# The second layer norm's statistics spread over three engines in a fused attention and feed-forward kernel

## What is computed

```
x = x + tanh(g_xattn) * attention(layernorm(x), ctx)      # 8 heads of 64, 77 context rows
y = fixed_quant(layernorm(x), 8, 4)                       # second layer norm: mean and variance of each row
h = relu(fixed_quant(y @ w1q.T + b1q, 8, 4))              # 1024 wide
x = x + tanh(g_ffn) * (h @ w2q.T + b2q)

layernorm(x) = (x - mean(x)) / sqrt(var(x) + 1e-5)
```

## Time and profile before

| what | value |
|---|---|
| median of 3 runs | 121.85 us (121.33, 121.85, 123.11) |
| span of the profiled execution | 119.5 us |
| TensorE, VectorE, ScalarE, GpSimd busy | 95%, 82%, 64%, 74% of the span |
| granted TensorE clock | full (2.4 GHz) in all slices |

### The profile page before, as it was taken

The page is one execution under the profiler, slowest core; times in us unless marked ns, Lnnn a source line. Parts: engine busy times, 40 slices in busy tenths (PEclk is TensorE's granted clock), DMA queues, the critical chain, the costliest instruction groups (busy, mean ns, idle before and its releaser), DMA issues.

```text
span 119.5 us, 2896 instructions
## 1 busy us (share of the span) xinstructions
PE 113.6 (95%) x1012; PEld 104.6 (88%) x1012; DVE 97.7 (82%) x223; ACT 76.7 (64%) x169; POOL 89.0 (74%) x160
## 2 busy tenths in 40 slices
PE   7699997999999999999999999999999999999990
PEld 2399975999799999999999999999999999998770
DVE  3039798999999999989999899999797969647981
ACT  4137775968779895995849394848483828448420
POOL 3003678588896988899898959894999998987620
PEclk9999999999999999999999999999999999999999
DMA  3999999100000000000020002000200020020204
GB/s 82 333 251 371 333 388 381 71 0 8 0 3 5 3 0 0 0 5 0 0 88 0 5 0 88 0 8 0 88 0 0 8 88 0 0 87 9 80 14 169
DMA packets 5328, 8.87 MB, mean 74 GB/s; under 512 B 1191, under 2 KB 2242, under 8 KB 5186
## 3 DMA queue, kind: packets, MB, share of 16 engines
q1 hardware_dynamic: 5082, 8.34, 19.8%
q10 hardware_dynamic: 232, 0.34, 0.8%
HBM read 6.59 MB, written 2.10 MB: 73 GB/s over the span
## 4 chain that ended last, share of the span: by engine, by line
PE 90%; DMA 4%; DVE 2%; ACT 1%; issue 1%; SPq 0%; DVEq 0%
PE of_ps L868 24%; PE sc_ps L832 23%; PE h_ps L900 12%; PE of_ps L915 8%; PE tr_ps L844 7%; DMA wk_sb<-in_L_xattn_Wk_dram 4%; PE tr_ps L814 2%; PE h_ps L787 2%; PE tr_ps L915 1%; PE sc_ps L915 1%; PE tr_ps L767 1%; PE of_ps L760 1%; PE tr_ps L760 1%; PE sc_ps L767 1%; DVE x_sb L659 1%; PE of_ps L881 1%
## 5 line engine op out<-in xcount | busy, mean ns | idle before, releaser
L832 PE MATMUL sc_ps<-a_sb,xT 128*128 128x308 f32 x192 | 31.2, 311 | 0.6 <-DVE probs L606 0.6
L868 PE MATMUL of_ps<-u_sb,pT 128*128 128x256 f32 x240 | 30.9, 281 | 0.0
L868 PEld LDWEIGHTS of_ps<-u_sb,pT 128*128 128x128 f32 x240 | 29.5, 188 | 0.1
L832 PEld LDWEIGHTS sc_ps<-a_sb,xT 128*128 128x128 f32 x192 | 27.5, 189 | 1.4 <-issue 1.2
L430 ACT ACTIVATE probs<-probs,rstd 128x616 f32<-128x616 f32 x16 | 13.1, 817 | 23.9 <-DVE probs L606 23.9
L473 ACT ACTIVATE hid_q<-h_ps,b1z 128x256 int8<-128x256 f32 x58 | 24.6, 495 | 3.6 <-PE h_ps L900 3.6
L292 POOL TENSOR_TENSOR probs<-probs,rden 128x616 f32<-128x616 f32 x16 | 19.5, 1221 | 2.0 <-DVE rden L616 2.0
L354 POOL CAST hid<-hid_q 128x512 bf16<-128x512 int8 x27 | 15.8, 611 | 2.0 <-ACT hid_q L473 2.0
L900 PE MATMUL h_ps<-x2T,w1T 128*128 128x256 bf16 x128 | 16.6, 273 | 0.1
L601 DVE TENSOR_REDUCE mx<-sc_ps 128x8 f32<-128x616 f32 x16 | 12.6, 787 | 4.1 <-PE sc_ps L832 4.1
L900 PEld LDWEIGHTS h_ps<-x2T,w1T 128*128 128x128 bf16 x128 | 12.4, 98 | 1.7 <-ACT x2T L479 0.3
(11 more groups left out here) (123 smaller groups left out, 177.4 us busy)
## 6 DMA issues: line engine op xcount, KB each, us to landing
w_sb<-in_L_ffn_w_dram SPq DMA_DIRECT2D x2, 1024.0 KB, 10.9
out_dram<-x_sb SPq DMA_DIRECT2D x7, 256.0 KB, 2.5
x_sb<-in_x_dram SPq DMA_DIRECT2D x4, 256.0 KB, 7.7
x_sb<-in_x_dram SPq DMA_DIRECT2D x1, 1024.0 KB, 9.7
wq_sb<-in_L_xattn_Wq_dram SPq DMA_DIRECT2D x1, 512.0 KB, 5.2
wv_sb<-in_L_xattn_Wv_dram SPq DMA_DIRECT2D x1, 512.0 KB, 7.4
wo_sb<-in_L_xattn_Wo_dram SPq DMA_DIRECT2D x1, 512.0 KB, 8.4
wk_sb<-in_L_xattn_Wk_dram SPq DMA_DIRECT2D x1, 256.0 KB, 4.2
```

Source lines behind the costliest of these rows:

```text
L832: ins = nc.tensor.matmul(sc_ps[:, a, 0:HALF], xT[:, T % 2, p, c, :], a_sb[:, q, T // TB, c, HALF * a:HALF * a + HALF], start=first, stop=last)
L868: ins = nc.tensor.matmul(attn_ps, pT[:, T % 2, p, P * c:P * c + P], u_sb[:, q, MC * (T // TB) + c, :], start=first, stop=last)
```

## The change

For tiles 3 to 14 the second mean and variance take another way. VectorE's residual instruction also writes the row sum from its accumulator (`residual_summed`), and `stats_second` is gone for these tiles. GpSimd makes minus the mean from the sum (`minus_mean_second`), then divides the probabilities of tile s+1, and only then normalises. ScalarE takes the squares of the centred rows with a row sum (`squares_second`), behind `xT_copy(s+3)` in its list, waiting for GpSimd's `nm2_ready`. GpSimd makes the variance from that sum (`sq2_ready`). For the other tiles the order stays.

```diff
+ACT_STATS = range(3, TILES - 1)
...
+            def minus_mean_second(T):
+                pool.wait_ge(x1_ready, T + 1)
+                nc.gpsimd.tensor_scalar(nm2[:, T % 2, :], sum2[:, T:T + 1], -1.0 / D, 1.0, ALU.mult, ALU.mult).then_inc(nm2_ready, 1)
...
             def normalise_second(T):
                 i = T % 2
                 if T == TILES - 1:
                     pool.wait_ge(ve2_dve, 2)
+                elif T in ACT_STATS:
+                    pool.wait_ge(sq2_ready, stats_on_act(T))
+                    nc.gpsimd.tensor_scalar(ve2[:, i, :], sq2[:, T:T + 1], 1.0 / (D * AQ * AQ), EPS / (AQ * AQ), ALU.mult,
+                                            ALU.add).then_inc(ve2_ready, 1)
                 else:
                     pool.wait_ge(mv2_ready, T + 1)
-                    variance_second(T)
+                    nc.gpsimd.tensor_scalar(ve2[:, i, :], mv2[:, i, 1:2], EPS, 1.0 / (AQ * AQ), ALU.add, ALU.mult).then_inc(ve2_ready, 1)
+                    nc.gpsimd.tensor_scalar(nm2[:, i, :], mv2[:, i, 0:1], -1.0, 1.0, ALU.mult, ALU.mult).then_inc(nm2_ready, 1)
...
-                if T + 2 == TILES - 1:
-                    softmax_scale(T + 2)
...
             for s in range(TILES):
-                if live(s - 1):
-                    normalise_second(s - 1)
-
-                if live(s + 2):
-                    softmax_scale(s + 1)
+                if live(s - 1) and s - 1 in ACT_STATS:
+                    minus_mean_second(s - 1)
+                    if live(s + 1):
+                        softmax_scale(s + 1)
+                    normalise_second(s - 1)
+                else:
+                    if live(s - 1):
+                        normalise_second(s - 1)
+                    if live(s + 1):
+                        softmax_scale(s + 1)
...
+            def squares_second(T):
+                act.wait_ge(nm2_ready, T + 1)
+                nc.scalar.activation(squares[:, :], x_sb[:, T, :], ACT.Square, bias=nm2[:, T % 2, 0:1],
+                                     accum_out=sq2[:, T:T + 1]).then_inc(sq2_ready, 1)
...
                 if live(s + 3):
                     xT_copy(s + 3)
+                if s - 1 in ACT_STATS:
+                    squares_second(s - 1)
...
+            def residual_summed(T):
+                dve.wait_ge(attn_psum, T + 1)
+                nc.vector.scalar_tensor_tensor(out=x_sb[:, T, :], in0=attn_ps, scalar=tg[:, 0:1], in1=x_sb[:, T, :],
+                                               op0=ALU.mult, op1=ALU.add, accum_out=sum2[:, T:T + 1]).then_inc(x1_ready, 1)
...
             for s in range(TILES):
-                if live(s - 1):
+                if live(s - 1) and s - 1 in ACT_STATS:
+                    residual_summed(s - 1)
+                elif live(s - 1):
                     residual(s - 1)
                     stats_second(s - 1)
```

More of the change, by code:

```diff
@@ L125, in flamingo_kernel @@
         nm2 = sb("nm2", [P, 2, 1])
+        sum2 = sb("sum2", [P, TILES])
+        sq2 = sb("sq2", [P, TILES])
+        squares = sb("squares", [P, D])
         yq = sb("yq", [P, 2, D], I8)
@@ L224, in flamingo_kernel @@
         ve2_dve = sem("ve2_dve")
+        nm2_ready, sq2_ready = sem("nm2_ready"), sem("sq2_ready")
         yq_ready, yT_psum, x2T_ready = sem("yq_ready"), sem("yT_psum"), sem("x2T_ready")
@@ L293, in softmax_scale, with stats_on_act @@
                                         ALU.mult).then_inc(probs_ready, 1)
+            def stats_on_act(T):
+                return len([t for t in ACT_STATS if t <= T])
+            def minus_mean_second(T):
+                pool.wait_ge(x1_ready, T + 1)
+                nc.gpsimd.tensor_scalar(nm2[:, T % 2, :], sum2[:, T:T + 1], -1.0 / D, 1.0, ALU.mult, ALU.mult).then_inc(nm2_ready, 1)
             def normalise_second(T):
@@ L298, in normalise_second @@
                     pool.wait_ge(ve2_dve, 2)
+                elif T in ACT_STATS:
+                    pool.wait_ge(sq2_ready, stats_on_act(T))
+                    nc.gpsimd.tensor_scalar(ve2[:, i, :], sq2[:, T:T + 1], 1.0 / (D * AQ * AQ), EPS / (AQ * AQ), ALU.mult,
+                                            ALU.add).then_inc(ve2_ready, 1)
                 else:
                     pool.wait_ge(mv2_ready, T + 1)
-                    variance_second(T)
+                    nc.gpsimd.tensor_scalar(ve2[:, i, :], mv2[:, i, 1:2], EPS, 1.0 / (AQ * AQ), ALU.add, ALU.mult).then_inc(ve2_ready, 1)
+                    nc.gpsimd.tensor_scalar(nm2[:, i, :], mv2[:, i, 0:1], -1.0, 1.0, ALU.mult, ALU.mult).then_inc(nm2_ready, 1)
+                if T < TILES - 1:
+                    pool.wait_ge(ve2_ready, T + 1)
                 nc.gpsimd.tensor_tensor(rstd2[:, i, :], ve2[:, i, :], mhalf[:, 0:1], ALU.pow).then_inc(rstd2_ready, 1)
-                if T + 2 == TILES - 1:
-                    softmax_scale(T + 2)
                 pool.wait_ge(rstd2_ready, T + 1)
+                if T < TILES - 1:
+                    pool.wait_ge(nm2_ready, T + 1)
                 if T >= 2:
@@ L309, in normalise_second @@
                                         ALU.add, ALU.mult).then_inc(yq_ready, 1)
[L311 to L315, removed]
             def a1_parts(c):
@@ L652, in stats_second @@
                 nc.vector.bn_stats(st2[:, T % 2, :], x_sb[:, T, :]).then_inc(st2_done, 1)
-                dve.wait_ge(st2_done, T + 1)
+                dve.wait_ge(st2_done, T + 1 - len([t for t in ACT_STATS if t <= T]))
                 nc.vector.bn_aggr(mv2[:, T % 2, :], st2[:, T % 2, :]).then_inc(mv2_ready, 1)
@@ L732, in _ @@
             last = (TILES - 1) % 2
-            dve.wait_ge(mv2_ready, TILES)
+            dve.wait_ge(mv2_ready, TILES - len(ACT_STATS))
             nc.vector.tensor_scalar(ve2[:, last, :], mv2[:, last, 1:2], EPS, 1.0 / (AQ * AQ), ALU.add, ALU.mult).then_inc(ve2_dve, 1)
```

## The result

| | median | runs | ratio to before, with 95% interval |
|---|---|---|---|
| kernel before | 121.59 us | 121.02 to 123.11, 4 runs | |
| changed kernel | 125.0 us | 124.2 to 125.85, 4 runs | 1.031 [1.026, 1.035] |
| changed kernel, measured again among the experiments | 123.87 us | 123.53 to 124.41, 6 runs, beside 121.31 | 1.0227 [1.0196, 1.0258] |

The change makes the kernel 2 to 3% slower. The ratios compare only runs within 1.5% of the fastest of their kernel; the medians take all runs. The second measurement is +2.75 us (0.0227 x 121.31) against the forecast's +2.55; the first is +3.7. Why they differ comes first, since it decides which trace is read.

What follows compares the result with a forecast made beforehand. TensorE, with 90% of the chain, was taken to bound the kernel. Losses of 1.3 (stages 4 to 6), 0.25 (stage 12) and 1.0 us (tail) sum to 2.55, added to 121.85 for 124.4 us; range 122.0 to 126.0.

Steps and rivals of the forecast that it cites:

- The ceiling: Whole kernel: at most some 0.4 us to gain, since TensorE is full; VectorE's saved time worth nothing by itself.
- Stages 4 to 6: Late minus the mean and added squares delay ScalarE's copy, so TensorE loses 1.3 us before attend(6).
- a lag of 0.11 and no slack: Stage 6 before the change: tile 4's copy ended at 54.78, attend(6) loaded its first weights at 54.89.
- Stages 7 to 11: ScalarE's copy shifts by 0.68 us within a slack of 0.71, so no loss.
- 0.03 to spare: Stage 8: margin in us left after the copy's shift of 0.68 out of 0.71 slack.
- Stage 12: A second bias in stage 11 makes the shift 1.37 us against a slack of 1.11: loss 0.25 us.
- The tail: After stage 15: tile 15's yq comes at 110.40 instead of 109.40, so the end moves by 1.0 us.
- A: Rival: only one of the losses, stages 4 to 6 or tail, comes; 122.3 to 124.0 us, chance 0.25.
- B: Rival: not slower, GpSimd runs ahead rather than idling before the division; 121.4 to 122.2 us, chance 0.15.
- C: Rival: the accumulator's read costs more, up to 0.39 us on ScalarE; 125.1 to 126.0 us, chance 0.15.
- D: Rival: ScalarE's squares need another activation table, two loads a tile; some 13 us more, 135 us, chance 0.03.

Runs made afterwards that it cites:

- e8: The changed kernel unaltered, measured again beside the kernel before: ratio 1.0227, +2.75 us.
- e4: Kernel before plus ScalarE's squares for tiles 3 to 14, waiting for the residual alone, result unused: ratio 1.0078, +0.95 us against the kernel before.
- e5: Changed kernel with minus the mean moved from GpSimd's list to VectorE's, right behind the residual: ratio 1.008, +0.97 us against the kernel before.
- e1: Changed kernel with the change for tiles 6 to 14 only: ratio 1.0144, +1.75 us against the kernel before.
- e2: Changed kernel with the change for tiles 6 to 10 only: ratio 1.0025, +0.30 us against the kernel before.
- e7: Changed kernel with the change for tiles 3 to 13 only, tile 14 left as before: ratio 1.0151, +1.83 us against the kernel before.
- e3: Kernel before with GpSimd's division ahead of the normalisation in stages 4 to 15, nothing else: ratio 1.0113, +1.37 us against the kernel before.
- e6: Changed kernel with minus the mean on VectorE, and the change for tiles 6 to 14 only: ratio 1.0012, +0.15 us against the kernel before.

## Why the prediction came out as it did

**The ceiling.** Right: VectorE's saved time could win nothing. Where the statistics were, VectorE now waits for the exponentials, 4.4 us in 9 waits. In stage 14 the reciprocal was to start 0.25 earlier, at 100.55 by before's clock; in e8 it starts at 102.41, and TensorE is 1.84 later there (its first weights of `attend(13)` load at 98.67, against 96.83 before), so at 100.57.

**Stages 4 to 6: 1.3 forecast, 1.39 measured.** By before's clock (0.07 taken off, by which stage 4 began later in e8): minus the mean at 53.95 (forecast 53.83), squares at 54.18 (54.08), the load at 56.28 (56.21). The working had the right chain. It did not name two things. First, some 1.0 of the 1.4 would be there without any wait, from ScalarE's time alone (e4, e5); I had folded that into "a lag of 0.11 and no slack". Second, TensorE also waits 0.23 for the widened half in stage 6; this lies ahead of the later wait for the copy and so inside the sum.

**Stages 7 to 11: 0 forecast, 0.07 measured.** The step to "0.03 to spare" was wrong, and the early loss hid it: when e1 and e2 took that loss away, 0.4 appeared in stage 8. The working gave every odd stage the rhythm of stage 14, with the division 1.92 us after the stage's start. But the kernel before already shows stage 7 slower:

```profile
57.19 0.81 ACT L430 ACTIVATE probs<-probs,rstd 128x616 f32<-128x616 f32 x1 [1.67 <-DVE probs L606]
```

These exponentials end 3.11 us after the first weights of `attend(6)` (54.89), those of stage 14 2.87 after `attend(13)`'s (98.89 + 0.81, against 96.83). So in e1 the division of stage 7 starts 4.26 us after that load (59.41, 55.15) where the forecast had 3.95 (56.92 + 1.92 - 54.89), 0.31 late. The list behind it takes another 0.12 more (59.41 to 65.22 is 5.81, the sum of the rows 5.69). Together that is the 0.4 of stage 8, less the 0.03.

**Stage 12: 0.25 forecast, 0.33 measured.** Squares at 91.19, less 1.53 of shift, is 89.66, against 89.57 forecast: GpSimd's list ran 0.09 longer than the sum of its rows. The division is the term that was too small: counted at 1.2, it takes 1.30 us in stage 11 to the start of the next instruction (84.48 to 85.78).

**The tail: 1.0 forecast, 0.97 measured.** With 1.84 of shift taken off: minus the mean 105.42 (forecast 105.40), squares 105.64 (105.65), the variance 106.33 (106.33), the hidden matmul's load 107.28 (107.37). `yq` starts at 110.66 (110.40) but takes 0.55 in place of 0.79, so TensorE gets it as forecast; that two errors of 0.25 cancel here is luck. e7 shows that tile 14's squares carry 0.8 of the loss. e3 loses as much in the tail without any squares, but by a list that is longer behind the division; e7, which keeps the change's own order through stage 14, loses 0.15 there. So e3's tail shows that a GpSimd list of that length has no slack, not what the order is worth within the change.

**The rivals.** A (only one loss) falls: both came, and either can be had nearly alone (e1, e7). B (not slower) falls: GpSimd idled before the division nine times. C (a dear accumulator read) falls: ScalarE's read lasts 0.19 but holds the next instruction back by 0.09 only (54.67 to 54.76), where 0.1 was taken. D falls, by the group of table loads in e8:

```profile
L531 ACT ACT_TABLE_LOAD x1 | 1.3, 1283 | 1.8 <-issue 1.8
```

One load, as before: Square brought none. The Trainium skill ("ScalarE: Activation LUTs", section "Table sets: the hidden batching unit") says that cheap functions lie in every set and names relu, copy, identity and abs. The trace fits that if Square is one of them, which the section does not say.

**The size.** Each of the four sums was within 0.1: in stages 7 to 11 because the early loss hid a wrong step, and in the tail because two errors cancelled. That part is luck; the waits in stages 6 and 12 came as worked out. The first measurement's further 1 us over the forecast (3.7 against 2.55) is not the change's, as far as its one profile tells: that run lost 1.8 us ahead of the first changed instruction. Its other three runs have no trace, so how much of their time was start-up stays open; two of them have spans of 122.3 and 122.8 us, close to those of e8's runs (121.7 to 122.6). The forecast called 2.44 us about what a measurement can tell from no change; e8's 2.75 [2.4, 3.1] does not settle on which side of that the change lies.

## What to carry to other kernels

Work moved to an engine that is "only 60% busy" is paid at the place in that engine's list where something is due: look for the consumer with no slack behind it, not at the busy share. When a one-value step becomes the input of another engine, ask what stands ahead of it in its own list; here moving minus the mean from the end of GpSimd's list to the engine that made its sum took away 1.7 to 1.8 of 2.75 us (by the stretches and by the times). A margin of a few hundredths is not cover, and an earlier loss can be what provides it.

## What was not expected of the hardware

The accumulator's read is an instruction of its own on both engines, and cheap: on VectorE (e8)

```profile
41.08 0.08 DVE L681 DVE_READ_ACCUMULATOR x_sb<-of_ps,tg,x_sb 128x1 f32 x1
```

it takes 0.08 us, and on ScalarE 0.19, of which 0.09 delay the next instruction (54.67 to 54.76, above). That it is an instruction of its own on VectorE agrees with the Trainium skill ("VectorE: DVE Perf Modes", section "Two Vector instructions with no wait between them").

The start-up varies from run to run: `attend` of stage 3 loaded at 37.13 (e5) to 39.73 us (the first profile), though TensorE's list is the same in all of them up to there. In the late ones (the first profile, e2, e6) TensorE's matmuls up to some 9 to 10 us run at half the pace, 1.03 against 0.53 us for four, the ratio of its two levels of 1.2 and 2.4 GHz; in the others they are at full pace by some 6.5 us at the latest. By the matmuls behind them (10.52 us in the first profile, 8.75 in the second) the whole 1.8 us is there. The row of the granted clock shows 1.00, the upper level, for this stretch in every run. That the clock was at its lower level is therefore an inference from the durations alone, and not shown. The Trainium skill ("TensorE: Matmul & The Clock Gate", section "What's actually happening") says that the number of slow matmuls at a kernel's start varies between runs of the same kernel; the traces agree as to the slow matmuls, but where it puts the cost under 1% of a span, here two runs differ by 1.8 of 124.1 us. Two variants some 2 us apart should therefore be compared by stretches.
